# The mid-row state copy of a selective scan, moved from ScalarE to VectorE

## The reference

```
def step(h, inp):
    u_t, d_t, B_t, C_t = inp
    dA = jnp.exp(d_t[..., None] * As)
    h = h * dA + (d_t * u_t)[..., None] * B_t[:, :, None, :]
    y = jnp.einsum('bkcn,bkn->bkc', h, C_t)
    return (h, y)
```

## Time and profile before

| | |
|---|---|
| median of three runs | 2097.51 us (2095.74 to 2097.67) |
| the profiled execution's own time | 2092.68 us |
| its span in the trace | 2090.9 us |
| busy: DVE / PE / POOL / ACT | 1645.8 / 1521.6 / 1437.7 / 853.0 us |
| the scan steps of the first pair | about 173 to 796 us of the span |
| the scan steps of the second pair | about 1032 to 1649 us |

### The profile page before, as it was taken

The page is one execution under the profiler, slowest core; times in us unless marked ns, Lnnn a source line. Parts: engine busy times, 40 slices in busy tenths (PEclk is TensorE's granted clock), DMA queues, the critical chain, the costliest instruction groups (busy, mean ns, idle before and its releaser), DMA issues.

```text
span 2090.9 us, 14512 instructions
## 1 busy us (share of the span) xinstructions
PE 1521.6 (73%) x3788; PEld 677.7 (32%) x3789; DVE 1645.8 (79%) x1640; ACT 853.0 (41%) x1288; POOL 1437.7 (69%) x535
## 2 busy tenths in 40 slices
PE   6754677676777676877377677577777775999997
PEld 2221232232222222622122232232222253555554
DVE  6699999997999997577999999999998674323232
ACT  3673544544444543357444544544444320111110
POOL 2498998987998984046799998999998512222221
PEclk9866888888898888888588888988888976999999
DMA  3155345336344321202834444334433273111110
GB/s 108 41 208 211 122 136 164 126 123 193 114 138 132 121 94 61 84 31 75 311 111 142 141 134 137 125 120 146 134 115 104 88 285 138 43 46 43 53 45 20
DMA packets 120144, 248.92 MB, mean 119 GB/s; under 512 B 20862, under 2 KB 33697, under 8 KB 116240
## 3 DMA queue, kind: packets, MB, share of 16 engines
q1 hardware_dynamic: 114960, 234.00, 33.7%
q0 software_dynamic: 5120, 14.21, 2.2%
HBM read 205.10 MB, written 44.60 MB: 119 GB/s over the span
## 4 chain that ended last, share of the span: by engine, by line
DVE 56%; PE 26%; issue 9%; ACT 3%; POOL 3%; DMA 3%; SPq 1%; DVEq 0%; POOLq 0%
DVE arena L845 30%; DVE arena L832 11%; PE psum L1222 9%; PE psum L1241 5%; DVE arena L793 3%; DVE arena L813 3%; POOL arena L454 2%; PE psum L1112 2%; DVE arena L811 2%; DMA arena<-bc_dram 2%; PE psum L1120 2%; PE psum L1082 1%; ACT arena L663 1%; DVE arena L807 1%; PE psum L1150 1%
## 5 line engine op out<-in xcount | busy, mean ns | idle before, releaser
L1120 PE MATMUL psum<-arena,ident 128*128 128x512 f32 x1536 | 822.0, 691 | 352.6 <-POOL arena L454 352.5
L454 POOL TENSOR_TENSOR arena<-arena 128x1536 f32<-128x1536 f32 x256 | 874.8, 3437 | 101.3 <-DVE arena L845 48.2
L845 DVE TENSOR_TENSOR_SCAN arena<-psum,arena 128x512 f32<-128x512 f32 x768 | 897.4, 1228 | 14.5 <-ACT psum L642 14.4
L642 ACT ACTIVATE psum<-arena 128x512 f32<-128x512 f32 x768 | 528.4, 691 | 655.4 <-DVE arena L845 655.4
L1120 PEld LDWEIGHTS psum<-arena,ident 128*128 128x128 f32 x1536 | 325.3, 219 | 847.1 <-POOL arena L454 489.9
L832 DVE TENSOR_TENSOR arena<-psum,arena 128x1536 f32<-128x1536 f32 x176 | 304.6, 1731 | 51.5 <-PE psum L1120 47.5
L439 POOL TENSOR_TENSOR arena<-arena 128x1536 f32<-128x1536 f32 x80 | 275.1, 3439 | 0.2 <-issue 0.2
L1222 PE MATMUL psum<-arena 128*128 x480 | 202.9, 559 | 0.0
L491 POOL TENSOR_TENSOR gap<-one 128x1 f32<-128x1 f32 x40 | 11.3, 284 | 211.1 <-DVE arena L1009 211.1
L716 ACT ACTIVATE arena<-psum 128x384 f32<-128x384 f32 x40 | 19.6, 490 | 301.6 <-PE psum L1213 301.6
L415 POOL TENSOR_TENSOR arena<-arena 128x1024 f32<-128x1024 f32 x16 | 50.0, 3126 | 109.0 <-ACT arena L554 107.0
(11 more groups left out here) (149 smaller groups left out, 1270.1 us busy)
## 6 DMA issues: line engine op xcount, KB each, us to landing
arena<-bc_dram SPq DMA_DIRECT2D x1024, 128.0 KB, 3.0
step_dram<-arena SPq DMA_DIRECT2D x16, 1536.0 KB, 6.3
arena<-step_dram SPq DMA_DIRECT2D x32, 768.0 KB, 8.0
arena<-in_x SPq DMA_DIRECT2D x8, 1536.0 KB, 8.7
arena<-in_w SPq DMA_DIRECT2D x6, 1876.0 KB, 10.9
t_dram<-arena SPq DMA_DIRECT2D x16, 386.0 KB, 4.1
arena<-in_w SPq DMA_DIRECT2D x4, 1536.0 KB, 14.6
z_dram<-arena SPq DMA_DIRECT2D x2, 1536.0 KB, 5.4
```

The costliest lines, as they stand in the source:

```text
L454: g.tensor_tensor(x, x, Cs[c % C_RING][:, None, :].to_broadcast([P, CG, HALF]), ALU.mult)\
L642: a.activation(dA[e % 2], steps[g % 2][0][:, j, :], ACT.Exp, scale=A[:, KORDER[kk], j, n:n + 1]).then_inc(s_dA, 1)
L845: v.tensor_tensor_scan(x, dA[(CG * c + j) % 2][:, ::way], x, 0.0 if first else state[:, n, j:j + 1], ALU.mult, ALU.add)\
L1120: ins = pe.matmul(bank[j], ident[:, :], X3[c % RING][:, j, :], start=False, stop=(n == NS - 1), skip_group_check=True)
```

## The change

The copy of the three state values of a step in a first half leaves ACT's stream, where it stood behind the second exp of the next step. It becomes a `tensor_scalar` (add 0.0) on DVE right behind the three scans of its own step, with a wait for these scans. POOL's wait on s_state stays, and so does DVE's own in the second halves.

```
@@ scalar
-                def keep_state(s):
-
-                    kk, _, _, n, _ = place(s)
-                    c = STEPS * p + s
-                    at = 0 if KORDER[kk] >= 2 else HALF - 1
-                    a.wait_ge(s_scan, CG * (c + 1))
-                    a.activation(state[:, n, :], X3[c % RING][:, :, at], ACT.Copy).then_inc(s_state, 1)
...
                     exp(s, 1)
-                    if s and place(s - 1)[4]:
-                        keep_state(s - 1)
                     exp(s, 2)
@@ vector
+                def keep_state(s):
+                    kk, _, _, n, _ = place(s)
+                    c = STEPS * p + s
+                    at = 0 if KORDER[kk] >= 2 else HALF - 1
+                    v.wait_ge(s_scan, CG * (c + 1))
+                    v.tensor_scalar(state[:, n, :], X3[c % RING][:, :, at], 0.0, None, ALU.add).then_inc(s_state, 1)
+
                 input_of(0)
                 for s in range(STEPS):
                     if s + 1 < STEPS and (s + 1) % NS not in BY_GPSIMD:
                         input_of(s + 1)
                     scans(s)
+                    if place(s)[4]:
+                        keep_state(s)
```

## The result

The changed kernel takes 2196.94 us (median of four runs, 2195.87 to 2199.67) against 2096.62 us before (four runs, 2092.74 to 2097.67). The ratio is 1.0484, with a 95% interval of 1.0466 to 1.0502: 100 us slower. The forecast was 2188 us in a range of 2112 to 2207. The profiled execution has a span of 2197.9 us, 107.0 more than the one before; it is the slowest of its four runs, and the profiled execution of the kernel before, at 2092.68 us, lies at the low end of its runs, so the traces show some 7 us more than the medians.

The account below looks back on a forecast made before the run. DVE, busiest engine and 56% of the chain, bounds the kernel. Group costs 2 x 12.7 + 4 x 11.7 + 8.2 + 10.7 = 91 us on 2092.7 give 2184, plus 4.8 for the median: 2188 us, range 2112 to 2207.

Parts of the forecast that it names:

- That DVE is held: On DVE, the copy waits until POOL's running instruction ends; 2188 us, for this mechanism alone 2168 to 2207; chance 0.74.
- the first rival: On DVE, three elements are not held, each copy costs only 0.18 us; 2117 us (2109 to 2131); chance 0.19.
- The holds, step by step: First halves: 2.0 us at n = 2, 5, 8, 11, 15; 0.27 at 3, 6, 9, 12; 14.0 a full half.
- The bare cost: On DVE, a copy without hold moves everything behind it by 0.17 to 0.18 us; bounds 0.10 and 0.30 us.
- What hides: Groups 2, 6, 12, 14 lose 2.27 us of cost in DVE's wait, 11.7 each; group 4 costs 8.2, group 10 10.7.
- the standstill: DVE stands still before the input of n = 5 in groups 2, 6, 12, 14; 3.17 us in group 2.
- a chain that the change doesn't touch: From the first scan of n = 2: exp, y_out, opening of the sums, first step's products; sets the standstill's end.
- both cases: Hold and no hold: in either, the profile would show ACT's busy time falling by 24 us.
- The earlier state: POOL gets the copy 0.2 us behind the scans, not about 1.0; worth nothing except in group 10, 0.8 us sooner.
- POOL's pace: First halves: POOL (13.6 us per three steps, DVE 13.4) decides, the earlier state gains 10 us; 2087 us; chance 0.03.
- Two turns of POOL before a held copy: Two POOL instructions pass before a held copy, certain once a group (n = 0); 54 us more, 2243 us; chance 0.04.
- the rate of line 791 alone: On DVE, small instructions at 0.45 ns an element run at line 791's two-a-cycle rate, so three elements are held too.

Follow-up runs that it names:

- The dummy run: Kernel before, copy still on ScalarE, plus a tensor_scalar of three constants to a spare tile on DVE behind each first-half step's scans, awaited by nobody; 2215.28 us.
- the run with pieces: Changed kernel with POOL's input of 1536 elements a partition cut into three instructions of 512; 2190.03 us.

## Why the prediction was right

**That DVE is held.** This was the deciding term, given 0.74, and it came about. Rows 9 had one tensor_scalar of 1024 elements beside a busy POOL; the copy of three behaves like it. The two runs that take the hold away and leave the copy (tensor_reduce, single elements) came to 2127 and 2132 us, which is the first rival's world.

**The holds, step by step.** n = 2, 5, 8, 11, 15: 2.0 us predicted, copies of 1.91 to 1.95 us measured in 39 of 40 cases. The fortieth is n = 5 of group 4, which the prediction took to be free because DVE stands still ahead of it; it took 0.17 us. n = 3, 6, 9, 12: asked for just before POOL's end, 0.22 to 0.25 us long. n = 0 of group 2: 1.8 predicted, 1.81 measured. Three steps in 15.8 to 15.9 us. Groups 0 and 8, where nothing hides, cost 12.9 us against 12.7.

**The bare cost was too small.** I took 0.18 us from the earlier trace rows. By the tensor_reduce run it is 0.25 to 0.28 us where an input follows and 0.19 where scans follow. The row that I chose had a successor without waits. An input carries waits of its own, starts 0.11 us after the copy's start (391.25 to 391.36) and not 0.07, and takes 0.02 us longer until its scans. The no-hold rival came out at 2117 us in the prediction; tensor_reduce, with the kernel before at 2093 beside it, at 2127. The prediction's low bound for the held case, 2168 us, takes the short copies' own 0.18 us out together with their holds; with them left in it is some 2175. Neither touches the forecast.

**What hides was over-credited.** In groups 2, 6, 12 and 14 I let 2.27 us each disappear in the standstill. By the rows it does, and the standstill is still there. But in three of these groups the stretch with the opening got longer by 0.9 to 1.3 us, at a lower granted clock, which the sum had at nothing. That is the sentence "by a chain that the change doesn't touch": the chain's work was untouched, its clock was not. The same holds for the second halves, where I wrote that the standstill stays: 5.8 us in all. With the 8 us of the openings the sum would have been 99. The medians lie 100 us apart, the two traces 107.

**ScalarE.** Its relief was worth nothing, as said, as far as the idle time tells: ACT idles 775 us before its exps now, 119 more than before. Its busy time fell by 16 us and not by the 24 that both cases named as a sign: 8 us of the copies lay over other instructions of ACT, and busy time counts that once. The earlier state was called worthless except in group 10. The dummy run shows otherwise for a held DVE: without it the cost is 18 us higher, because POOL's instruction then ends later.

**The other rivals.** POOL's pace did not decide before the change: DVE has no wait for a slot in mid group. Two turns of POOL before a held copy were not seen: all 47 held copies of the changed kernel end 0.02 to 0.03 us after the POOL instruction under way. But the prediction priced this rival wrongly. It called a ready successor on POOL certain at n = 0; yet POOL's next instruction is each time the C multiply of the same step, which waits for this very copy, so in the changed kernel it could not have come about. What refutes it is the run with pieces and the run with the dummy, where a POOL instruction was ready and the held one still had its turn first.

**A reading of the rate.** The prediction took 0.45 ns an element from the earlier trace rows for the rate of line 791 alone. That line's 0.81 us are 0.79 ns an element, its fixed part included, so the two do not show one rate. No term of the sum hung on it, only the guess that three elements are treated as 1024 are, which the run itself decided.

## What to carry to other kernels

Before a small VectorE instruction goes beside a busy GpSimd, look in the trace for an instruction of the same kind at a quiet and at a busy moment. Its price is not its length but the rest of whatever GpSimd runs, and it repeats in the rhythm of the two engines. If it must go there, a form that isn't held (here a tensor_reduce, or single elements) costs about a third of the 100 us here. The rest of the price is paid wherever the receiving engine sets the pace; when TensorE set it, the same change cost 13 us.

## What was not expected of the hardware

- A tensor_scalar of two or three elements is held by GpSimd, for up to 1.98 us, and one of a single element is not (0.16 us at most). The Trainium skill, "Vector Engine (DVE) Microarchitecture Reference", section "5.1 Performance modes — why throughput varies by op and dtype", has two elements from SBUF in the two-port mode; the run with two agrees (812 ns in the mean, 2198.74 us for the kernel).
- A held instruction of VectorE goes between two back-to-back instructions of GpSimd, and GpSimd loses nothing visible by it: the dummy ends at 392.96 us, beside POOL rows that start at 389.50 and 392.89.
- An fp32 matmul with weights of only 8 columns took as long as one with 128: 597 ns against 612 ns a record in the same run.
